# A transformer layer on eight cores: the copies of the queries and keys move from the head of a head pair's block to the tail of the block before

## What is computed

```python
x = x + 0.5 * ffn(layernorm(x), U1, V1, b1, U2, V2, b2)
x = x + attn(layernorm(x), Q_w, Q_b, K_w, K_b, V_w, V_b, O_w, O_b)
x = x + 0.5 * ffn(layernorm(x), U1, V1, b1, U2, V2, b2)

# attn: 16 heads of 64 columns, causal
q = einsum('bpm,hmd->bphd', x, Q_w) + Q_b      # k, v alike
logits = einsum('bqhd,bkhd->bhqk', q, k) / 8
scores = softmax(where(causal, -1e5, logits))
out = einsum('bqhd,hdm->bqm', einsum('bhqk,bkhd->bqhd', scores, v), O_w) + O_b
# ffn: low rank, gelu(x U1 V1 + b1) U2 V2 + b2
```

## Time and profile before

| What | Value |
|---|---|
| median of 2 runs | 1983.18 us (1982.87 to 1983.49) |
| the profiled execution, its own time | 1981.44 us |
| its span on the slowest core (core 7) | 1979.9 us |
| spans of the eight cores | 1961.3 to 1979.9 us |
| PE busy | 1560.8 us, 79% |
| DVE busy | 564.4 us, 29% |
| ACT busy | 556.6 us, 28% |
| mean granted clock of PE, core 7 | 0.755 |

### The profile page before, as it was taken

How to read it: one execution, slowest core, us unless ns; L and a number is a source line. 1 busy time by engine, 2 the same in 40 slices (tenths; PEclk the granted TensorE clock), 3 DMA queues, 4 the chain that set the end, 5 groups by cost and what they waited for, 6 DMA issues and landing times. The chain is left out here.

```text
span 1979.9 us, 17903 instructions; the slowest of 8 cores (1961.3 to 1979.9 us)
## 1 busy us (share of the span) xinstructions
PE 1560.8 (79%) x5640; PEld 416.2 (21%) x5640; DVE 564.4 (29%) x947; ACT 556.6 (28%) x615; POOL 106.6 (5%) x117
## 2 busy tenths in 40 slices
PE   2489999548659969789698797986978797499997
PEld 0022222112112212112121121221211132122222
DVE  2522201652231322413214133141231124601211
ACT  1232232110013333433333333333344301232222
POOL 0100000000000100001000010000100011100000
PEclk7598899759875868658677585686875698597997
DMA  8400000301130010100200102001000024201111
GB/s 258 126 0 0 1 0 1 107 13 36 31 80 1 11 43 1 40 14 1 54 1 11 43 1 54 0 11 33 1 22 0 11 74 142 72 0 43 43 43 43
DMA packets 74440, 72.69 MB, mean 37 GB/s; under 512 B 20935, under 2 KB 59991, under 8 KB 73326
## 3 DMA queue, kind: packets, MB, share of 16 engines
q1 hardware_dynamic: 74350, 71.54, 12.7%
HBM read 50.49 MB, written 12.58 MB: 32 GB/s over the span
## 5 line engine op out<-in xcount | busy, mean ns | idle before, releaser
L753 ACT ACTIVATE pt<-p_big 128x1024 bf16<-128x1024 f32 (+3 forms) x320 | 286.2, 894 | 594.5 <-PE p_big L714 338.8
L708 PE MATMUL p_big<-qgA,kgA 65*128 65x512 bf16 (+3 forms) x320 | 149.6, 467 | 117.9 <-ACT pt L753 56.7
L598 ACT ACTIVATE hb<-p_big 128x1024 bf16<-128x1024 f32 x128 | 130.8, 1023 | 312.8 <-PE p_big L521 310.9
L519 PE MATMUL p_big<-pb,v1b 128*128 128x512 bf16 x512 | 160.7, 397 | 15.8 <-DVE pb L556 15.8
L667 PE MATMUL p_big<-pt,v_pair 128*64 128x512 bf16 (+3 forms) x320 | 158.1, 494 | 0.0
L670 PE MATMUL p_big<-pt,v_pair 128*64 128x512 bf16 (+3 forms) x320 | 157.4, 492 | 0.0
L714 PE MATMUL p_big<-qgB,kgB 65*128 65x512 bf16 (+3 forms) x320 | 156.1, 488 | 0.0
L663 PE MATMUL p_big<-pt,ones_bf 128*1 128x512 bf16 (+3 forms) x320 | 154.4, 482 | 0.0
L659 PE MATMUL p_big<-pt,ones_bf 128*1 128x512 bf16 (+3 forms) x320 | 145.6, 455 | 0.3
L529 PE MATMUL p_big<-hb,u2b 128*128 128x512 bf16 x512 | 136.8, 391 | 4.7 <-ACT hb L598 4.7
L230 PE MATMUL p_big<-xb_s,ones_bf 128*1 128x512 bf16 x96 | 49.9, 520 | 79.8 <-DVE xb_s L251 79.2
(11 more groups left out here) (149 smaller groups left out, 1596.2 us busy)
## 6 DMA issues: line engine op xcount, KB each, us to landing
wstage<-u SPq DMA_DIRECT2D x40, 256.0 KB, 5.5
wstage<-v SPq DMA_DIRECT2D x40, 256.0 KB, 4.4
x<-xT SPq DMA_DIRECT2D x8, 1024.0 KB, 11.7
outT<-x SPq DMA_DIRECT2D x32, 256.0 KB, 2.3
wstage<-vw SPq DMA_DIRECT2D x16, 256.0 KB
vscr<-vb_s SPq DMA_DIRECT2D x32, 128.0 KB
v_pair<-vscr SPq DMA_DIRECT2D x8, 512.0 KB
wst<-ow SPq DMA_DIRECT2D x8, 512.0 KB, 4.2
```

The source lines that it names most:

```text
L519: tensor.matmul(psl, v1b[:, rc, 128 * fc:128 * (fc + 1)], pb[:, c % 2, rc, :], start=(rc == 0), stop=False)
L598: ACT.inc(scalar.activation(hb[:, 2 * (fp % 2):2 * (fp % 2) + 2, :], psl.rearrange("p (a b) -> p a b", a=2), AF.Gelu_apprx_tanh))
L708: mm = tensor.matmul(p_big[:, 0:w], kgA[:, ksl], qgA[:, lo:hi], start=True, stop=not first)
L753: ch["XA"].inc(scalar.activation(pt[:, :, i % 2, 0:w], p_big[:, 0:1024].rearrange("p (a b) -> p a b", a=2)[:, :, 0:w], AF.Exp))
```

## The change

The six copies for pair p+1 are taken from the head of its block and put at the tail of SP's stream in pair p's block. There SP waits for pair p's last score matmuls (PA and PB at N2, the number of steps) and for all writes of qp1, kp1 and u_row (WS at the new mark `ws_end`). The copies of pair 0 go into the small block in which POOL writes the rows of ones. PE's wait at a block's head, and the gate on writing u_row, now name the count of DMX at the block's start, which holds the copies issued in the block before.

```diff
-                                           act0=act0, dmx_gate=dmx0 + 96, xa0=xa0)
+                                           act0=act0, dmx_gate=dmx0, xa0=xa0)
...
                 @blk.tensor
                 def _(tensor):
-                    tensor.wait_ge(DMX.h, dmx0 + 96)
+                    tensor.wait_ge(DMX.h, dmx0)
                     tensor.wait_ge(LSL[4].h, v_mark)
...
                         ct["v_marks"][0] = LSL[4].v
-                    DMX.inc(sync.dma_start(qgA[0:64, :], qp_r[0:64, :]), 16)
-                    DMX.inc(sync.dma_start(qgB[0:64, :], qp_r[64:128, :]), 16)
-                    DMX.inc(sync.dma_start(kgA[0:64, :], kp_r[0:64, :]), 16)
-                    DMX.inc(sync.dma_start(kgB[0:64, :], kp_r[64:128, :]), 16)
-                    DMX.inc(sync.dma_start(kgA[64:65, :], u_row[0:1, 0, :]), 16)
-                    DMX.inc(sync.dma_start(kgB[64:65, :], u_row[0:1, 1, :]), 16)
                     if p + 1 < NP:
...
                         sync.wait_ge(LD.h, LD.v)
+                    if not last:
+                        qp_n, kp_n = ct["qp1"][(p + 1) % 2], ct["kp1"][(p + 1) % 2]
+                        sync.wait_ge(ch["PA"].h, pa0 + N2)
+                        sync.wait_ge(ch["PB"].h, pb0 + N2)
+                        sync.wait_ge(ch["WS"].h, aux["ws_end"])
+                        DMX.inc(sync.dma_start(qgA[0:64, :], qp_n[0:64, :]), 16)
+                        DMX.inc(sync.dma_start(qgB[0:64, :], qp_n[64:128, :]), 16)
+                        DMX.inc(sync.dma_start(kgA[0:64, :], kp_n[0:64, :]), 16)
+                        DMX.inc(sync.dma_start(kgB[0:64, :], kp_n[64:128, :]), 16)
+                        DMX.inc(sync.dma_start(kgA[64:65, :], u_row[0:1, 0, :]), 16)
+                        DMX.inc(sync.dma_start(kgB[64:65, :], u_row[0:1, 1, :]), 16)
...
-                        dve_urow=dve_urow, pool=pool, pj0=pj0)
+                        dve_urow=dve_urow, pool=pool, pj0=pj0, ws_end=ws0 + 14)
...
                         gp.memset(ct["qgA"][64:65, :], 1.0)
                         gp.memset(ct["qgB"][64:65, :], 1.0)
+
+                    @blk.sync
+                    def _(sync):
+                        DMX.inc(sync.dma_start(ct["qgA"][0:64, :],
+                                               ct["qp1"][0][0:64, :]), 16)
...
```

More of the change, by code:

```diff
@@ L1374, in _ @@
                         gp.memset(ct["qgB"][64:65, :], 1.0)
+                    @blk.sync
+                    def _(sync):
+                        DMX.inc(sync.dma_start(ct["qgA"][0:64, :],
+                                               ct["qp1"][0][0:64, :]), 16)
+                        DMX.inc(sync.dma_start(ct["qgB"][0:64, :],
+                                               ct["qp1"][0][64:128, :]), 16)
+                        DMX.inc(sync.dma_start(ct["kgA"][0:64, :],
+                                               ct["kp1"][0][0:64, :]), 16)
+                        DMX.inc(sync.dma_start(ct["kgB"][0:64, :],
+                                               ct["kp1"][0][64:128, :]), 16)
+                        DMX.inc(sync.dma_start(ct["kgA"][64:65, :],
+                                               ct["u_row"][0:1, 0, :]), 16)
+                        DMX.inc(sync.dma_start(ct["kgB"][64:65, :],
+                                               ct["u_row"][0:1, 1, :]), 16)
                 for p in range(NP):
```

## The result

Over 43 runs of the changed kernel and 42 of the one before, taken side by side, the medians are 1994.59 and 1985.36 us. The medians are over all executions; the ratio leaves out those in which the cores of a die ran slower at a lower granted clock, which some executions do whatever the kernel. It is 1.0041, with a 95% interval of 1.0024 to 1.0057: 8 us slower (5 to 11), well under the 2% bound. The forecast was +8.4 us. That it is so close is partly luck, as the traces show: the boundaries cost more than reckoned, and the clock, which was no part of the sum, gave some of it back.

A forecast was written before the change was run, and what follows sets the result against it. Attention was taken as bound by PE and ACT handing over tiles, with PE idle about 8.1 us at each boundary. Boundaries +11.4 and first pair -3.0 gave +8.4 us on 1983.18: 1991.6 us, range 1974 to 2002.

The forecast's parts named there:

- What was late in the wait's place: At each boundary, six issues at SP's tail hold the barrier, ACT starts 3.47 us later, and DVE's row releases PE.
- the chain: At a boundary, ACT's last-chunk logarithm, then DVE's reciprocal parts, which L679 needs; late only 2.3 us less than the copies.
- The rival in which the issues don't hold the barrier: At the boundaries, ACT's start stays put despite SP's issues: -17.0 us in all, 1966 us; chance 7%.
- The size of that term: At the seven boundaries: 1.24 us lost at the first, 2.03 at the seventh, 11.4 in all (8.7 to 14.2).
- the time of leaving the block: At a boundary, from the last engine's end to ACT's start: 0.30 us, read behind PE and used behind SP.
- The first pair: At pair 0, copies issued in POOL's small block, ahead of v_pair's load, let PE start 3.0 us earlier (1.7 to 5.0).
- v_pair's landing: At pair 0, the time from issue to landing of v_pair's load, taken as 5.0 us between 3.1 and 6.3.
- Costed at nothing: At a block's head, SP's loads of v_pair and weights come 1.4 us later, and u_row's gate is already met: no cost.
- The clock: Within the pairs, a rival: shifted starts against the clock's changes add 9 us to the sum, giving 2001 us; chance 6%.

The follow-up runs named there:

- the second set of runs: The changed kernel run again without any edit, against the kernel before in the same session: ratio 0.9998 (0.9958 to 1.0038).
- the three profiles with the uncovered table load: Changed kernel with ACT's and DVE's last-chunk work moved into the pair's own block, profiled twice (0.9960, 0.9902), and once with one more 1 KB copy (0.9955).

## Why the prediction was right, and where it wasn't

What was late in the wait's place. Right, and by the predicted path: first issue 0.15 us behind the last score matmul (0.10 forecast), ACT 5.48 behind it (5.2), DVE's row as the releaser. Two more issues at the tail moved ACT and PE by their own time; taking the chain out from behind the barrier moved PE by 3.5 us; with only two issues at the tail ACT came 0.3 us late in place of 3.9. The rival in which the issues don't hold the barrier has fallen. The Trainium skill ("DMA: Bandwidth & Descriptors", section "Issuing engines are not separate DMA queues") says that the sequencer's time to start a DMA is usually small relative to the DMA itself. This case differs: issuing takes 4.8 us at a place where the wait for the copies is 7.8 in all.

The size of that term. 1.24 us were forecast at the first boundary and 1.58 measured; 11.4 in seven, and 12.7 measured on the mean of the cores. The step that was too small is the time of leaving the block: I took the 0.30 us that ACT needs behind PE, but behind SP it is 0.52 at this boundary (0.65 on core 0, and 0.52 to 0.66 on all). Seven times 0.22 is 1.5 us and covers the miss. What differed between boundaries evened out as well: before, PE's start varied from 9.00 to 9.92 behind the last score matmul with the copies; now six of seven are at 11.13 to 11.18.

The first pair. 3.0 us were forecast; 4.0 measured on core 7 and 3.4 on the mean. The step is v_pair's landing, taken as 5.0 us between bounds of 3.1 and 6.3; it took 4.2.

Costed at nothing: the later loads of v_pair and weights. Right: in the changed kernel SP issues them at 703.75, and nobody waits for them.

The clock. Wrong in sign: the forecast's rival had it only as an addition of up to 9 us, and as a term of the sum it wasn't there. In both profiles of the changed kernel PE spends some 54 us less at 1.2 GHz within the bodies, which are 4 to 5 us shorter, and over all executions the mean granted clock is 0.771 in place of 0.759 or 0.760. With it the traces' sum is +5, not +8.4, and on the mean of the cores the second set of runs has +2.2 us (3.8 either way), with a ratio of 0.9998 for the slowest core. The first set's medians say 8, with an interval from 5; so a true value near the lower end would fit all. That the forecast lay on the first ratio is luck to this extent: a boundary term 1.3 too small, a first-pair term 0.4 too small and a missing -4.4 in the bodies lie within what the slowest of eight cores varies by anyway.

Still open is why the clock favours one kernel's pairs over another's. That it belongs to the kernel is shown, and that one added issue can change it. But the length of the boundaries doesn't order it: 69.3 us of them went with a mean granted clock of 0.775, 68.1 with 0.770, 72.6 with 0.761, 80 with 0.759, and 92.8 and 101.5 with 0.771 and 0.770.

## What to carry to other kernels

A transfer that is issued before a barrier isn't free: the barrier waits for the issuing, and everything at the head of the next block waits for the barrier. Before moving work across one, write down what else is at the head behind the wait you remove (here a chain only 2.3 us less late), and move only as many issues as fit under the engine that reaches the barrier last, with room for the barrier's own price (here two of six, which still cost ACT 0.3 us); or move the chain too, and look what then comes first on each engine. And in a kernel whose clock comes and goes, count the gain at the place itself as well as in the total, since the stretches between can give back or add as much; and compare the mean of the cores over many executions before reading a cause out of one profile.

## What the runs showed that I had not expected

How much the clock makes of the same code. Leaving out the three profiles with the uncovered table load, the bodies went from 894 to 904 us while their time at 1.2 GHz went from 480 to 550, and one kernel gave 894 and 900 in two profiles. With the 9 us of the load taken off, two of those three are at 901 and 906 for 535 and 572, near the same line: about 1 us of time for 8 or 9 us at 1.2 GHz, with single profiles up to 3 us off it. That is probably since PE and ACT wait for each other in these steps, so that only a part of PE's longer matmuls shows; that was not tried by itself.

Where ACT's one table load of a block falls. Before, it cost nothing, since the copies came 2.3 us later than the chain that it stands in. In front of the first exponential it delays PE by 1.28 us a pair. In the changed kernel it stands in the chain that sets PE's start, so there too its 1.28 us are probably paid at each boundary; that was not tried by itself. Moving the logarithm moved it without a line in the diff that says so.

The barrier's own price depends on who comes last: 0.29 or 0.30 us from PE's end to ACT's start, and 0.52 to 0.66 from SP's. So SP's last issue decides even where it ends a little before PE does, as with the two query copies.

An issue's time on SP has little to do with its bytes: at the boundaries 1 KB took 0.50 to 0.60 us, 4 KB 0.58 to 1.29, 256 KB 0.46 to 1.12, and v_pair's load of 512 KB 0.40 to 0.53. By these figures what helps there is fewer copies, not smaller ones.
